# Decoder kernel on one core: two halves of a masked score step, a maximum and a drain are put at other places in the engines' hand-written order

## The reference, cut to what matters

```python
def _encoder_layer(x, ...):              # L0_attn, four times
    h = _layernorm(x, ln1_s, ln1_b)
    q, k, v = (h @ Wq + bq), (h @ Wk + bk), (h @ Wv + bv)   # 16 heads of 8
    attn = _linear_attention(q, k, v)    # qp = elu(q) + 1, kp = elu(k) + 1
    x = x + (attn @ Wo + bo)
    h = _layernorm(x, ln2_s, ln2_b)
    return x + relu(h @ W1 + b1) @ W2 + b2
...
def _L1_attn_ref(x, ...):                # top-k attention, TOP_K = 64
    scores = einsum('bhqd,bhkd->bhqk', q, k) / sqrt(D_HEAD)
    _, idx = top_k(scores, TOP_K)
    logits = where(knn_mask, scores, -inf)
    return x + einsum('bhqk,bhkd->bhqd', softmax(logits), v) @ w_out_w.T + b
...
x = x + _L0_attn_ref(_layernorm(x), ...)     # encoder
x = x + _L0_xattn_ref(_layernorm(x), ctx, ctx, mask, ...)
x = x + _L0_ffn_ref(_layernorm(x), ...)
x = x + _L1_attn_ref(_layernorm(x), ...)     # top-k attention
x = x + _L1_xattn_ref(_layernorm(x), ctx, ctx, ...)
x = x + _L1_ffn_ref(_layernorm(x), ...)      # eight experts
```

## Time and profile before

| what | us |
|---|---|
| median of three runs | 1383.07 (1380.2 to 1387.07) |
| the profiled execution, its own time | 1385.35 |
| its span | 1383.6 |
| PE / PE weight loads busy | 1050.0 (76%) / 694.4 (50%) |
| DVE busy | 949.1 (69%) |
| ACT busy | 678.8 (49%) |
| POOL busy | 485.3 (35%) |
| chain that ended last, by engine | PE 45%, DVE 31%, POOL 8%, ACT 8%, issue 7% |

### The profile page before, as it was taken

The page is one execution under the profiler, slowest core; times in us unless marked ns, Lnnn a source line. Parts: engine busy times, 40 slices in busy tenths (PEclk is TensorE's granted clock), DMA queues, the critical chain, the costliest instruction groups (busy, mean ns, idle before and its releaser), DMA issues.

```text
span 1383.6 us, 17897 instructions
## 1 busy us (share of the span) xinstructions
PE 1050.0 (76%) x5082; PEld 694.4 (50%) x5082; DVE 949.1 (69%) x3098; ACT 678.8 (49%) x1774; POOL 485.3 (35%) x461
## 2 busy tenths in 40 slices
PE   4988846555768288875865689789998856888999
PEld 3776713334446166653542334333444444666887
DVE  7555588987488788888867768535666576665332
ACT  4444437433667256664437544256667634633322
POOL 4333347411655145555146300433343413311100
PEclk9999968756888578886657799889998986989999
DMA  4001010000000000000010011011110120222443
GB/s 140 27 25 30 29 32 1 1 0 1 13 20 15 1 22 10 18 9 1 1 54 1 1 38 46 23 46 56 48 47 24 50 77 26 83 77 77 130 144 115
DMA packets 41762, 53.88 MB, mean 39 GB/s; under 512 B 6448, under 2 KB 20672, under 8 KB 41664
## 3 DMA queue, kind: packets, MB, share of 16 engines
q1 hardware_dynamic: 41488, 52.24, 12.2%
q0 software_dynamic: 176, 0.53, 0.1%
HBM read 51.71 MB, written 1.05 MB: 38 GB/s over the span
## 4 chain that ended last, share of the span: by engine, by line
PE 45%; DVE 31%; POOL 8%; ACT 8%; issue 7%; DVEq 1%; DMA 0%; POOLq 0%; ACTq 0%
PE psum L1747 7%; PE psum L1758 6%; PE psum L1733 6%; ACT far L1040 3%; PE psum L1514 3%; PE psum L1824 2%; PE psum L1333 2%; PE psum L1410 2%; DVE near L2055 2%; PE psum L1831 2%; POOL Wk L711 2%; PE psum L1490 2%; DVE h L1969 2%; DVE nmax L2139 1%; DVE S L2560 1%
## 5 line engine op out<-in xcount | busy, mean ns | idle before, releaser
L2267 DVE TENSOR_TENSOR big<-psum,qe 128x512 f32<-128x512 f32 x106 | 72.9, 688 | 173.5 <-ACT qe L1193 78.0
L1040 ACT ACTIVATE far<-far,half_far,fmul 128x128 bf16<-128x128 bf16 x256 | 103.0, 486 | 50.7 <-DVE hit L2042 50.7
L1193 ACT ACTIVATE qe<-psum 128x512 f32<-128x512 f32 x106 | 62.1, 595 | 119.9 <-PE psum L1747 119.8
L1733 PE MATMUL psum<-big,wexp 128*128 128x256 f32 (+1 forms) x340 | 116.9, 460 | 0.0
L2055 DVE MAX8 near<-Wk 128x8 f32<-128x128 f32 x512 | 102.9, 274 | 0.0
L668 POOL TENSOR_SCALAR veps<-mv 128x4 f32<-128x4 f32 x35 | 8.7, 248 | 261.9 <-DVE mv L1961 261.9
L766 POOL TENSOR_TENSOR Wk<-Wk,far 128x1024 f32<-128x1024 f32 x32 | 67.9, 2126 | 60.7 <-ACT far L1040 60.7
L1733 PEld LDWEIGHTS psum<-big,wexp 128*128 128x128 f32 x340 | 69.6, 205 | 29.9 <-issue 20.8
L1410 PE MATMUL psum<-ident,Wk 128*128 128x128 f32 x256 | 48.2, 356 | 47.1 <-POOL Wk L711 43.8
L1758 PE MATMUL psum<-xin,wexp 128*128 128x512 f32 x128 | 69.9, 629 | 16.8 <-DVE far L2267 9.3
L1747 PE MATMUL psum<-xin,wexp 128*128 128x512 f32 x128 | 75.2, 672 | 2.5 <-DVE vaug L2707 1.5
(11 more groups left out here) (359 smaller groups left out, 2875.5 us busy)
## 6 DMA issues: line engine op xcount, KB each, us to landing
wexp<-in_mg SPq DMA_DIRECT2D x48, 256.0 KB, 2.6
wexp<-in_mu SPq DMA_DIRECT2D x48, 256.0 KB, 2.9
wexp<-in_md SPq DMA_DIRECT2D x48, 256.0 KB, 3.0
w<-in_aw SPq DMA_DIRECT2D x8, 256.0 KB, 2.9
w<-in_w2a SPq DMA_DIRECT2D x8, 256.0 KB, 2.5
wqkv<-in_aw SPq DMA_DIRECT2D x8, 192.0 KB, 2.2
ctxt<-in_ctx SPq DMA_DIRECT2D x5, 256.0 KB, 4.2
xin<-in_x SPq DMA_DIRECT2D x4, 256.0 KB, 3.1
```

The source lines that it names most:

```text
L1040: ins = act.activation(far[t][:, hd, :], far[t][:, hd, :], ACT.Identity, bias=half_far[:, 0:1], scale=fmul[t][:, hd:hd + 1])
L1733: mm = pe.matmul(bank(4)[:, 0:w], wd[l % 2][:, c + j, :], hid_of[k >= EARLY][k % CH][:, j * w:(j + 1) * w], start=first and j == 0, stop=l ...
L2267: dve.tensor_tensor(hid_of[k >= EARLY][k % CH], bank(U_BANK[k]), sg_of[k >= EARLY][k % 2], ALU.mult).then_inc(hu_done, 1)
```

## The change

In the turns 0 to 8 of the merged stage: on PE the second half of `turned_scores(b-2)` moves behind the down products; the third quarter of `outputs` moves ahead of the transposes of `attend(b+2, "input")`, and `settled_rows` ahead of its projections. On ACT the second exponentials move behind the last penalties and the copy of `attend(b+1, "attended")`. On DVE `maxima(b)` moves from the end of the turn to the place between the statistics of kind "F" and their normalization, `mark_dropped` behind that normalization, and `unsettled_rows` ahead of the projections. In the drain: what turn 9 did for sequence 7 moves forward; its turned scores and exponentials go between the context's transposes, keys and values, a preset of S goes with them, and its outputs go between the two context queries. POOL's and SP's orders stay as they are, instruction for instruction.

```diff
@@ ACT merged_turn @@
-                if old:
+                if old and b <= NB:
                     exponentials(b - 2, 0)
                 if b == NB + 1:
-                    context_queries(1, (0,))
+                    context_queries(1)
                 if fed:
                     feed(b, 1)
-                if old:
-                    exponentials(b - 2, 1)
-                if b == NB + 1:
-                    context_queries(1, (1,))
                 if here:
                     penalties(b, range(11, H))
                 if step:
                     attend(b + 1, "attended")
+                if old and b <= NB:
+                    exponentials(b - 2, 1)
@@ ACT beside_encoder @@
-                    if b == NB + 1:
-                        act.wait_ge(drop_done, NB)
-                        preset_scores((NB - 1) % 3)
@@ ACT context_keys @@
                 for s in SL:
+                    if hf == 1:
+                        exponentials(NB - 1, s)
+                    if hf == 1 and s == 1:
+                        act.wait_ge(drop_done, NB)
+                        preset_scores((NB - 1) % 3)
                     act.wait_ge(pk_mm, nth(s, hf * 2 + 1))
@@ PE cross_queries @@
-            def cross_queries(s, hf):
+            def cross_queries(s, hf, meanwhile=None):
...
                 hT_tr(s, hf * NLN + LN_B, CROSS_BANKS[hf][s][2])
+                if meanwhile is not None:
+                    meanwhile()
                 pe.wait_ge(hT_done, both(s, hf * NTR + (TR_B + 1)))
@@ PE merged_turn @@
-                if old:
+                if old and b <= NB:
                     turned_scores(b - 2, 0)
                 if b == NB + 1:
-                    cross_queries(0, 1)
+                    cross_queries(0, 1, lambda: outputs(NB - 1, 0))
+                    cross_queries(1, 1, lambda: (outputs(NB - 1, 1), outputs(NB - 1, 2)))
+                    outputs(NB - 1, 3)
...
-                if old:
-                    turned_scores(b - 2, 1)
-                if b == NB + 1:
-                    cross_queries(1, 1)
                 if step:
                     attend(b + 1, "attended")
                 if fed:
                     feed(b, "down")
+                if old and b <= NB:
+                    turned_scores(b - 2, 1)
                 if step:
                     attend(b + 1, "output")
...
                 if new:
                     scores(b + 1, 1)
+                if old and b <= NB:
+                    outputs(b - 2, 2)
                 if after:
                     attend(b + 2, "input")
-                if old:
-                    outputs(b - 2, 2)
+                if old and b <= NB:
                     outputs(b - 2, 3)
+                if before:
+                    settled_rows(b - 1)
                 if after:
                     attend(b + 2, "projections")
-                if before:
-                    settled_rows(b - 1)
@@ PE context_turned @@
                 for s in SL:
+                    if hf == 1:
+                        turned_scores(NB - 1, s)
                     pe.wait_ge(ctxT_done, nth(s, hf + 1))
@@ DVE merged_turn @@
                 if step:
                     attend(b + 1, "output")
+                if here:
+                    maxima(b)
+                if step or b == -1:
+                    step_normalize("F", b + 1)
                 if before:
                     mark_dropped(b - 1)
-                if step or b == -1:
-                    step_normalize("F", b + 1)
                 if old:
                     head_outputs(b - 2)
+                if before:
+                    unsettled_rows(b - 1)
                 if after:
                     attend(b + 2, "projections")
-                if before:
-                    unsettled_rows(b - 1)
-                if here:
-                    maxima(b)
                 if before:
                     settle(b - 1)
```

## The result

The changed kernel takes 1394.26 us (median of 6 runs, 1393.72 to 1395.25) where the kernel before took 1383.09 beside it (6 runs, 1378.04 to 1387.07): a ratio of 1.0094 with a 95% interval of 1.0075 to 1.0113. It is slower, by about 1%. A repeat on another occasion gave 1396.39 against 1378.43, 1.0129 (1.0110 to 1.0148). The forecast was 1389.5: right in its sign and its range, too small in its size.

The account below looks back on a forecast made before the run. It took DVE's work and waits to bound a turn. Added 3.5 + 22.5 + 1.5, removed 16.6, 1.1 and 3.5, gave +6.3 us: 1391.7 from the profiled execution, 1389.4 from the median; predicted 1389.5, range 1375 to 1398.

Parts of the forecast that it names:

- keys, queries and the signed scores: At five turn ends, GpSimd's signed scores block DVE's keys and queries in SBUF: 4.5 us each, 22.5 us added.
- F root waits: DVE's six waits of 1.25 us for GpSimd's root before the F normalization go: 7.5 us removed.
- A root waits: Three DVE waits of 0.37 us for GpSimd's A root go, as the second penalties come earlier: 1.1 us removed.
- down products: DVE's waits for PE's down products in the turns shrink, as these run before the second turned scores: 2.3 us removed.
- projections: PE finishes the projections before DVE reaches kk, so DVE's three waits in turns 1 to 6 go: 2.6 us removed.
- settled rows: DVE's two waits for PE's settled rows in turns 1 to 6 go: 0.9 us removed.
- register load of `settle`: On DVE, no longer under the reduction: 0.5 us at five turn ends, 1.0 at turn 6's, 3.5 us added.
- splitting beside normalization: POOL's five small instructions meet DVE's F normalization and `mark_dropped`: 0.3 us a turn, 1.5 us added.
- drain: DVE's 6.44 us wait for the outputs of sequence 7 shrinks, as half run between the queries: 3.5 us removed.
- Rival A: Faster: at the turn ends the keys get through before the signed scores L757; 1372.5 us, chance 0.2.
- C: Same: keys go ahead of L757, only queries are blocked, and the drain gains 5 us; 1382 us, chance 0.2.
- rival B: Slower: PE at its lower clock ends its products 5 us behind DVE in turn 5; about 1400 us, chance 0.1.

Follow-up runs that it names:

- e13: The changed kernel, unchanged, profiled once more: 1396.39 us, ratio 1.0129 to the kernel before.
- e3: The changed kernel, with GpSimd's signed scores also waiting for the queries of the same turn: 1375.09 us, ratio 0.9971 to the kernel before.
- e2: The kernel before with only DVE's new turn order and PE's settled rows moved: 1397.36 us, ratio 1.0109.
- e5: The kernel before, POOL's order alone changed: the five instructions splitting the maxima stand behind the next turn's signed scores: 1406.11 us, ratio 1.0200.
- e6: The changed kernel with PE's and ACT's moves inside the turns undone, DVE's order and the settled rows kept: 1397.33 us, ratio 1.0143.
- e15: The changed kernel with signed scores waiting for the queries, second turned scores and exponentials placed as before: 1376.01 us, ratio 0.9973.
- e11: The changed kernel with DVE's order, settled rows and the outputs' place as before; drain and turned scores behind the down products stay: 1384.44 us, ratio 1.0029.
- e12: The changed kernel with DVE's order, settled rows, turned scores and exponentials as before; drain and the outputs' move stay: 1375.71 us, ratio 0.9971.

## Why the prediction was right and where it was wrong

DVE's time in turns 0 to 6 by the prediction's own terms, in us against before:

| term | forecast | after | e13 |
|---|---|---|---|
| keys, queries and the signed scores | +22.5 | +23.1 | +23.0 |
| F root waits | -7.5 | -7.5 | -7.5 |
| A root waits | -1.1 | -1.1 | -1.1 |
| turn 0 | -2.2 | -4.1 | -2.2 |
| down products | -2.3 | -1.1 | -1.8 |
| projections | -2.6 | +1.0 | +3.5 |
| settled rows | -0.9 | -0.9 | -0.9 |
| register load of `settle`, five turn ends | +2.5 | +1.9 | +1.9 |
| end of turn 6 | +1.0 | +2.0 | +2.0 |
| `thresholds`, L2077 | 0 | -1.5 | -1.5 |
| splitting beside normalization | +1.5 | 0 | 0 |
| sum / length of the turns, measured | +10.9 | +11.8 / +11.0 | +15.4 / +15.3 |
| turns 7 and 8 | -1.1 | -1.7 | -1.8 |
| drain | -3.5 | -2.6 | -2.5 |

The first row of after is 9.1 of waits for ACT at five turn ends, 8.7 by which five keys exceed 0.68, and 5.25 by which five queries exceed 0.71. The measured lengths are 272.0 and 276.3 less 261.0. The forecast's 3.5 for the register load is split into five turn ends and the end of turn 6.

**The deciding term was right,** in place and in size: 4.6 us per turn end where 4.5 was taken, from turn 0 of before. Rival A asked whether L757 begins before the keys. It does, within 0.1 us of the end of the sides in turn 5, and e3 shows about what A would have been: 4.8 us below before, where A said 10.7. C is refuted by the keys of 1.8 to 2.7. The Trainium skill's page SBUF — State Buffer, section Who interferes with whom, says that issue order decides who blocks; e2, e3 and e5 show both orders, with keys or queries of 0.7 on one side and up to 4.1 us on the other.

**The projections were wrong,** and they are the step that failed: "I get the projections from 579.5 to 583.3 [...], where DVE reaches kk at 583.8 to 584.1. So the waits for projections (2.6) and settled rows (0.9) go [...]. The cover is thin, half a microsecond." It was not there. DVE waits for the projections in turns 2 to 5 of both profiles, 0.55 to 1.16 us in after and 0.49 to 2.44 in e13, so that one of the prediction's own signs of being wrong, a wait of over 1 us at L2365, is met. Counted from the end of `at`, the forecast had the projections begin after 14.3 us (579.5 less 565.24). They begin after 15.3 in turn 3 of after, 16.8 in turn 5, and 17.6 in turn 5 of e13; and DVE is at kk after 17.9, not 18.6 to 18.9, where it waits 1.28 for the down products.

Two things were missing on PE's side. First, the forecast moved exponentials and scores back by 1.7 us, which uses up the 1.54 us for which PE of before idled ahead of the transposes, and the quarter of the outputs that now stands there has no idle time left to run in. The row of before, and that quarter in after:

```profile
576.36 1.11 PE L1333 MATMUL psum<-ident,h 128*128 128x128 f32 x4 [1.54 <-DVE h L2354]
```

```profile
588.15 1.35 PE L1516 MATMUL psum<-vaug,wexp 128*128 128x10 f32 x8
```

From `at` to kk PE is now busy all but 0.3 to 0.4 us in turns 2 to 5, so whatever makes it slower reaches DVE. Second, PE did not run at the durations of before. In turn 5 of after it idled 2.73 us for `at`, and its next products were slow:

```profile
575.52 1.11 PE L1333 MATMUL psum<-ident,at 128*128 128x128 f32 x4 [2.73 <-DVE at L2390]
576.43 4.74 PE L1618 MATMUL psum<-w,big 128*128 128x128 f32 x32
```

These down products are 4.74 instead of 3.74, and DVE's wait of 2.7 for them is the largest of its six; the other five are 1.28, as forecast. In turn 5 of e13 there was no such gap, and the down products took 3.84. There the second scores were slow instead, 2.07 us for 1.13, and the wait at kk is the longest of all:

```profile
587.90 2.07 PE L1474 MATMUL psum<-kblk,qT 32*128 32x512 f32 x4
594.51 3.44 PE L1565 MATMUL psum<-wqkv,hT 128*128 128x256 f32 x8
```

Over the eight turns the waits at kk follow the granted clock of the time from `at` to kk: 0.5 to 0.7 us at 0.84 and 0.85, 1.1 to 1.2 at 0.82, 2.10 at 0.77 and 2.44 at 0.76 (in turn 5 of after, also at 0.76, DVE spent part of it in its wait of 2.7). So with PE full, its clock goes far to set the wait. That the turned scores, put into this time, are what fills it, is shown by e6 and e15, where they stand as before: DVE's waits for the projections are 0.3 and 0, as forecast for the change. The argument against rival B, "PE is continuously fed from 561 on", did not hold in either way: PE had a gap in after, and in e13 it was slow without one. B's mechanism is there in part: projections and down products together miss their terms by 4.8 us in after and 6.6 in e13, where B took 10.

**Smaller terms were off both ways,** and hid part of this in the sum. The splitting beside the normalization cost DVE nothing (1.11 us for L2358, 1.12 in the earlier trace rows); POOL paid, with 2.46 for L796 under `mark_dropped`. The Trainium skill (SBUF — State Buffer, section Who interferes with whom) says that a tensor_scalar can hold the shared pair, from which the prediction had worked out a loss of up to 5 us; these rows do not show one. The register load cost 1.2 us instead of 0.2 ahead of the long branch in turn 2, and 0.9 at the other ends together. At the end of turn 6 DVE waits 2.03 us for PE's L1548 in both profiles; the reduction had stood there before, with no wait behind it, and the forecast had 1.0. In `thresholds` a gain came that nobody had forecast: L2077 took 0.67 us in turns 3 to 5 of before, in turn 5 beside POOL's L849, and 0.17 in all turns of after. In the drain DVE waits 2.71 for the channel products instead of 1.1, and 1.15 for the outputs where the earlier trace rows had 6.44; with the rest it gave 2.6:

```profile
703.38 0.69 DVE L2257 SCALAR_TENSOR_TENSOR qe<-psum,rowe 128x512 f32<-128x512 f32 x1 [2.71 <-PE psum L1719]
...
713.47 0.26 DVE L2151 RECIPROCAL zden<-psum 128x16 f32<-128x16 f32 x1 [1.15 <-PE psum L1516]
```

**And the sum was set against one profile.** In the first profile of after it came true almost to the digit, 6.7 for 6.3, by errors that cancel; the second shows 11.0, the medians 11.2 and 18.0. The 4 us between the two profiles are turn 0 (1.9) and the projections (2.5), less 0.7 at the down products. So the failed step accounts for 3.6 to 6.1 us inside the stretch; the rest of what the medians show lies outside it, and its cause was not found. "Later stages are the same program, shifted" is true of the program and not of its time, which varies by 7 us from execution to execution.

## What to carry to other kernels

Engines that meet only through semaphores in the program can still meet in SBUF, as the keys did here with GpSimd's signed scores (up to 2.69 us instead of 0.68). An instruction that seems late in one engine's stream may be the gate that keeps another engine's operands free: before moving it, ask which long instruction it holds back, and with whom that one collides. If the early order is wanted all the same, give the long instruction a wait on the real condition; one wait here was worth about 20 us. And work that fills a wait of PE is not idle filler: taken out of a gap that was 1 us, it made one of 2.7 in five turns of e11, and it now stands in the row of products for which DVE waits next. A cover of half a microsecond, worked out with one turn's durations, is no cover where the granted clock of that part of a turn is anything from 0.76 to 0.85.

## What the runs showed that I had not expected

After an idle time of 2.74 us PE's next 5.6 us had a granted clock of 0.74, with 4.72 us for the 32 rows of the down products, where after 1.04 us of idling the clock was 1.00 and the same rows took 3.74 (e11 and e12, turn 1). The gap alone does not settle it: in e11's turns 5 and 6 a gap of the same length was followed by rows of 3.74. Nor is a gap needed: in turn 5 of e13 the granted clock is 0.50, the level of 1.2 GHz, from 587.9 to 594.5, though PE had idled only 0.4 us in all since 571.3. What it ran from 585.7 until the clock fell were outputs, sixteen rows of 128x10 (L1516).

When L757 ended, POOL's next instruction (L855, 1.7 us) came in ahead of the queries at each of the five turn ends of after where the keys were locked out, though DVE had the queries next in line. With POOL's instructions following each other without a gap, DVE got one operation through in between, and from the start of the 3.6 us L757 to the end of the queries 5.8 us passed.
